# An adaLN layer on one core: the routed tiles' second products move to two banks of their own, and the feed-forward's first products end two tiles earlier

## What is computed

```python
h = layernorm(x) * (1 + ca) + sa
x = x + ga * attention(h)                     # 16 heads of 16, causal
h = layernorm(x) * (1 + cb) + sb
shared = silu(h @ w1.T) * (h @ w2.T) @ w3.T   # 1024 hidden
top2 = top_k(sigmoid(h @ router.T) + bias, 2) # 8 experts, 256 hidden each
routed = sum over the two experts of (silu(h1) * h2 * gate) @ w3[e].T
x = x + gb * (shared + routed)
```

## Time and profile before

| | us |
|---|---|
| runs (three) | 2202.20, 2202.41, 2206.81; median 2202.41 |
| the profiled execution, its own time | 2220.47 |
| its span, first to last instruction | 2218.6 |
| TensorE busy | 1999.8 (90%) |
| VectorE busy | 1626.2 (73%) |
| ScalarE busy | 1067.9 (48%) |
| GpSimd busy | 799.4 (36%) |
| mean granted TensorE clock | 0.953 of full |

### The profile page before, as it was taken

How to read it: one execution, slowest core, us unless ns; L and a number is a source line. 1 busy time by engine, 2 the same in 40 slices (tenths; PEclk the granted TensorE clock), 3 DMA queues, 4 the chain that set the end, 5 groups by cost and what they waited for, 6 DMA issues and landing times.

```text
span 2218.6 us, 47132 instructions
## 1 busy us (share of the span) xinstructions
PE 1999.8 (90%) x17686; PEld 1057.9 (48%) x17686; DVE 1626.2 (73%) x4438; ACT 1067.9 (48%) x1401; POOL 799.4 (36%) x811
## 2 busy tenths in 40 slices
PE   5778889999999899989999999999998988999995
PEld 2223334344444444434443444354444477788773
DVE  6887778776877697768777877787778366655475
ACT  1555544554555455545454545455553545444431
POOL 1110142133223422342234323322323447876653
PEclk8788889998999999999999999899998999999997
DMA  3246220102011201120202020102010446787696
GB/s 124 97 162 200 77 66 22 50 21 71 18 42 38 73 16 49 34 70 16 59 29 65 21 63 26 58 24 60 27 48 21 157 92 114 126 172 121 152 282 203
DMA packets 109661, 175.64 MB, mean 79 GB/s; under 512 B 14576, under 2 KB 80376, under 8 KB 108288
## 3 DMA queue, kind: packets, MB, share of 16 engines
q1 hardware_dynamic: 82848, 136.63, 20.5%
q0 software_dynamic: 26592, 36.00, 8.7%
HBM read 76.43 MB, written 70.44 MB: 66 GB/s over the span
## 4 chain that ended last, share of the span: by engine, by line
PE 60%; DVE 27%; ACT 4%; issue 3%; POOL 3%; DMA 2%; another core or an unknown queue 1%; SPq 1%; POOLq 0%; ACTq 0%; DVEq 0%
PE bank L1794 11%; DVE bank L1247 8%; DVE max_part L1241 8%; PE bank L1846 8%; PE bank L1826 6%; PE bank L1757 5%; PE bank L1709 5%; PE misc L1780 5%; PE bank L1733 4%; PE pv L1780 3%; PE bank L1837 3%; PE bank L1873 2%; PE bank L1719 2%; ACT arena L1050 2%; POOL sum L938 1%
## 5 line engine op out<-in xcount | busy, mean ns | idle before, releaser
L1050 ACT ACTIVATE arena<-bank 128x1024 f32<-128x1024 f32 (+1 forms) x640 | 592.8, 935 | 448.9 <-PE bank L1757 419.9
L1247 DVE CUSTOM_DVE_ANT_0 bank<-bank,mask 128x512 f32<-128x512 f32 (+3 forms) x1024 | 472.2, 520 | 69.1 <-PE bank L1733 58.3
L880 POOL TENSOR_SCALAR_AFFINE_SELECT arena<-arena 128x512 f32<-128x512 f32 x256 | 170.0, 671 | 711.5 <-ACT arena L1050 711.0
L1794 PE MATMUL bank<-feat_parts,ffn_sb 128*128 128x512 f16 x1536 | 371.8, 391 | 7.5 <-ACT arena L1050 3.2
L1241 DVE TENSOR_REDUCE max_part<-bank 128x2 f32<-128x1024 f32 x256 | 312.4, 1220 | 25.8 <-PE bank L1733 23.5
L1757 PE MATMUL bank<-arena 50*128 50x256 f16 (+1 forms) x2560 | 244.7, 271 | 69.7 <-DVE max_part L1241 23.2
L1733 PE MATMUL bank<-arena 48*128 48x512 f16 (+3 forms) x1536 | 233.3, 349 | 57.7 <-DVE max_part L1247 19.4
L938 POOL DMA_INDIRECT sum<-arena,feat x142 | 232.2, 1635 | 136.8 <-DVE arena L1473 65.5
L944 POOL TENSOR_TENSOR hidden<-silu_h,hidden 128x512 f16<-128x512 f32 x128 | 155.8, 1220 | 249.3 <-ACT hidden L1083 248.3
L1780 PE MATMUL misc<-arena,v_sb 128*32 128x256 f32 (+1 forms) x3072 | 236.9, 382 | 1.0 <-POOL arena L880 0.9
L1794 PEld LDWEIGHTS bank<-feat_parts,ffn_sb 128*128 128x128 f16 x1536 | 142.2, 100 | 199.7 <-issue 38.6
(11 more groups left out here) (211 smaller groups left out, 2476.6 us busy)
## 6 DMA issues: line engine op xcount, KB each, us to landing
arena<-parts SPq DMA_DIRECT2D x384, 64.0 KB, 2.2
feat<-lists SPq DMA_DIRECT2D x71, 265.0 KB
sum<-feat_parts SPq DMA_DIRECT2D x9, 1024.0 KB, 6.3
rows<-x SPq DMA_DIRECT2D x8, 1024.0 KB, 5.6
x_sb<-x SPq DMA_DIRECT2D x16, 512.0 KB, 6.5
sum<-norm SPq DMA_DIRECT2D x14, 512.0 KB, 3.3
ffn_parts<-hidden SPq DMA_DIRECT2D x8, 768.0 KB, 4.1
arena<-ffn_parts SPq DMA_DIRECT2D x8, 768.0 KB, 7.0
```

The costliest lines, as they stand in the source:

```text
L880: gp.affine_select(p, p, [[0, GH], [1, P]], ALU.is_ge, 0.0, 0, -1).then_inc(masked, 1)
L1050: sc.activation(to[:, :, lo:QC], of[:, :, lo:QC], ACT.Exp, scale=SCALE / QK_SCALE ** 2).then_inc(exp_done, 1)
L1247: last = vec.tensor_tensor_reduce(scored, scored, mask[:, 512 - nk:], scale=1.0, scalar=NEG, op0=ALU.add, op1=ALU.max, accum_out=max_part[ ...
L1794: last = mm(to[:, 512 * m:512 * m + 512], w_up[s][W_PART[i]][:, f, m * RH + h * P:m * RH + (h + 1) * P], feat_parts[:, A_PART[i], f, c * 5 ...
```

## The change

The y products of tile i (`ty`) no longer take a tile of the planned three; they go to `attended[i % 2]`, and TensorE waits for that bank's last reader by hand: for tiles 0 and 1 for the attention's last two steps, from then on for `y_ready` of tile i-2. `ty` goes out of BUSY and READ, so that the plan of all other steps in the end comes out anew. In that new plan the steady tiles alternate as xr(i+3) in the tile that tup(i) had, tup(i+2) in the one that xr(i+2) had; where before tup(i+2) followed tup(i+1), xr(i+3) followed xr(i+2) and ty(i) followed ty(i-1), each in its own tile. In the stretch with the router and the ranks the new plan gives tup(10) the tile of router 0 just ahead of it, tup(14) that of rank 0, tup(15) that of router 1, tup(19) that of rank 1 and tup(22) that of count 1 (the last as before); tup(8) keeps following tup(7).

LATE_FFN goes from 19 items to 22, spread over the tiles 52 to 68 instead of 52 to 70: all 16 ups and the last low part now lie ahead of ty(68), and four downs alone follow the last tile. The tiles 52, 55, 58, 62 and 65 get two items. `down` 0 comes in tile 58's step, behind tup(60) and ahead of ty(58); before it came in tile 61's, behind xr(64).

```diff
-LATE_FFN = len(END_FFN) - 7
+LATE_FFN = len(END_FFN) - 4
 FFN_FROM = 52
-FFN_AT = [FFN_FROM + n * (ALL_TILES - FFN_FROM) // LATE_FFN for n in range(LATE_FFN)]
+FFN_AT = [FFN_FROM + n * (ALL_TILES - 2 - FFN_FROM) // LATE_FFN for n in range(LATE_FFN)]
...
-            if n == 4:
+            if n == 1:
                 put([("own", 0)])
...
-        "qk": 46, "v": 46, "turn_out": 5, "max_turn": 8, "rank": 4, "count": 1, "mods": 60, "xr": 9, "tup": 28, "ty": 15}
+        "qk": 46, "v": 46, "turn_out": 5, "max_turn": 8, "rank": 4, "count": 1, "mods": 60, "xr": 9, "tup": 28}
...
-        "qk": 30, "v": 17, "max_turn": 14, "rank": 6, "count": 4, "mods": 16, "xr": 18, "tup": 18, "ty": 9}
+        "qk": 30, "v": 17, "max_turn": 14, "rank": 6, "count": 4, "mods": 16, "xr": 18, "tup": 18}
...
-                        out_tile(at[0], buffer_of(v, ("ty", at[0])))
+                        out_tile(at[0], attended[at[0] % 2])
...
-                elif kind == "ty":
-                    pe.wait_ge(y_ready, at_tile(at[0]))
...
-                        tile_down(at[0], take(b, v, ("ty", at[0])))
+
+                        i = at[0]
+                        if i < 2:
+                            pe.wait_ge(o_ready, at_step(B - 1, STEPS - 2 + i))
+                        else:
+                            pe.wait_ge(y_ready, at_tile(i - 2))
+                        tile_down(i, attended[i % 2])
```

## The result

The change makes the kernel slower: 2209.85 us against 2201.36 (medians of 20 runs each), ratio 1.0042 with a 95% interval of 1.0031 to 1.0052, so some 9 us. (One run of the kernel before took 5258.82 us; the median hardly feels it.) The forecast was 2200.0, with a range of 2192.5 to 2206.5.

A forecast was written before the change was run, and what follows sets the result against it. TensorE with VectorE, and close by GpSimd's chain of adds, bound tiles 12 to 30. Tile 67's add, 2164.07 + 12.95 + 1.0 - 4.5 = 2173.5, plus 42.7 gave 2216.2 profiled, 2200.0 us as median; range 2192.5 to 2206.5.

The forecast's parts named there:

- Part 1: New banks, tiles 0 to 25: 7.5 us faster by TensorE and VectorE alone, capped and taken as -4.5 us.
- Together 5.9: Tiles 0 to 25: us added because tup(10), tup(15), tup(14) and tup(19) stand right behind a router or rank.
- rival C: Slower: tups behind router, rank or count, tup(10) to tup(22), tie TensorE to VectorE's order; 2207.5 us, chance 0.13.
- The clock: Tiles 0 to 25: 1.7 us regained from a tup slowed by the lower clock after a 2.00 us wait.
- The cap of 4.5 us by the chain of adds: Around tile 21: GpSimd's unbroken adds limit the gain of the new banks to 1.0 + 3.5 us.
- Part 2: Steady tiles: no change, 0 us, since TensorE is full there.
- Part 3: Feed-forward among the tiles: down 0 waits 3.2 us for its low part in its new place, +1.0 us in all.
- Part 4: The tail: five ups moved ahead cost +12.95 us; from tile 67's add to the end 42.7 us against 54.5.
- The rule on descriptors: Tail adds: GpSimd can't write descriptors while VectorE holds the shared port; some 0.6 us more per pair, not summed.
- rival D: Tail adds or landings slower, first_loads 24 us after tile 67's add: 2204.6 us, no change, chance 0.15.
- B: Tiles 0 to 25: the cap doesn't hold, the full 7.5 to 13.4 us come, 2197.0 to 2191.1 us; chance 0.25.
- E: Tail: the 9.3 us idle was only a shadow of the loads, moved ups do nothing; 2198.9 us, chance 0.05.

The follow-up runs named there:

- e1: The change's banks and plan with the feed-forward schedule of before, against the kernel before: 2206.13 against 2196.90 us, ratio 1.0045.
- e5: The change plus a third buffer for the tiles' rows, against the kernel before: ratio 1.0002.
- e14: The new banks with the old feed-forward schedule and a third row buffer, without raised reading costs, against the kernel before: ratio 0.9992.
- e16: New banks, planner's reading costs of 45, third row buffer and old feed-forward schedule, against the kernel before: 2180.21 against 2200.04 us, ratio 0.9910.
- e2: The kernel before with only the change's feed-forward schedule, second products still in the ring of three: ratio to before 1.0010.
- e12: The kernel before with only a third buffer for the tiles' rows: ratio to before 0.9956.
- e9: The change with the planner's reading costs of router, rank and count raised to 45 in the end: 2198.85 us, ratio to before 0.9992.
- e17: The kernel before with the third row buffer and the planner's reading costs of 45, second products still in the ring: ratio to before 0.9962.

## Why the prediction was wrong

**Part 1 is the step that failed: -4.5 forecast, +7.9 measured** (e1: 9.2 us by the medians). TensorE's time from the first second product to tile 30's can be split into waits of over 0.15 us and the rest: 14.8 + 144.4 before, 21.0 + 146.1 after. By its terms:

- The old waits, 13.4 to go: right. 13.4 us of waits for L1461 and L1473 in this stretch became 0.5; the 1.7 that I left for the table was too cautious by 1.2.
- "Together 5.9" for the new waits behind readers: 12.3 in the trace; before had 1.0 at count 1 and 0.2 at rank 0, so 11.1 are new. Each tup's shift was priced rightly: tup(10) began 43.31 us after the first second product where it had begun 42.15, +1.2 (forecast +1.5), tup(14) 5.4 later (forecast 4.4 with tup(10)'s). What was wrong is the sum: I took the price once off the gain, while the gain itself was waited away as well. TensorE came early to each reader (tile 7's second products were 2.2 us ahead) and waited that lead away there. That is rival C, whose price was to be "twice that if what was gained is waited for again"; I gave it 0.13.
- The clock: I had booked 1.7 as won, since one wait of 2.00 us goes. But three tups now ran slow behind waits of 4.02, 3.66 and 2.26: 5.09, 3.94 and 4.29 us to the next second products where 2.62 is usual. The rest column says +1.7 lost net, 3.4 from my term.
- Row loads, 8.0 us in this stretch: absent from the sum. Before had one such wait, 2.1 us for tile 2's rows ahead of the first second product, and none behind it; it is the line that the earlier trace rows leaves out, `PE bank L1805 <- DMA feat<-lists: 2.1, 1, 2.1`. The prediction asked for the cover of the chain of adds and not for that of the loads, which hang on VectorE's copy of ids two tiles back. e5 and e14 show that they are a cost of their own, though a part of it comes back as other waits.

Together: 5.2 for the readers, 3.4 for the clock, 8.0 for rows, less 1.2, is 15.4, and from the -7.5 that I had for TensorE and VectorE alone that gives the measured +7.9.

- The cap of 4.5 us by the chain of adds: wrong, and it didn't show in the change only because nothing was won. In e16 tile 30 is 12.1 us earlier although tile 22's add is only 3.1 us earlier (127.7 against 130.8): two banks and four output buffers lie between them, and tile 30's add may come 14.5 us behind its second products. The steady tiles, 4.38 us each for TensorE and some 3.7 for a pair of adds, close the gap later.

**Part 2**, 0: the 21 steady tiles took 91.9 us instead of 92.8. Right within a microsecond.

**Part 3**, +1.0: the stretch from tile 51 to tile 67 grew by 14.3, 12.95 of it the ups, so +1.3. The wait of down 0 was 3.33 (forecast 3.2), against 2.47 in the earlier trace rows.

**Part 4**, the tail of 42.7: 44.3 was measured. first_loads started 19.1 after tile 67's add (forecast 19.4). What was off is the fifth load: I had the eight loads in one row by their rate, but the fifth waits for tile 70's add to land, and that took 6.83 us from its issue, beside the first four loads; the earlier trace rows have 4.72 for tile 68's in the kernel before. VectorE began its last eight instructions at +31.1 instead of +29.5. Ups and tail together cost +4.0 where I had +2.15; e2's ratio gives 2.2, its medians 4.2.

**The rule on descriptors.** The two adds of tile 68 took 1.82 and 2.08 us, those of tile 69 1.55 and 2.17, and both of tile 70's, with no output made beside them, 1.55. So pairs beside the output making are longer by 0.8 and 0.6 us; the forecast had some 0.6. Whether that is the rule's doing isn't shown: the Trainium skill (SBUF — State Buffer, the "DVE blocks DMA" trap) tells it of VectorE operations in a two-port mode, with a `tensor_copy` as its example, and the output making here is a `tensor_tensor`. These pairs took 3.88 and 3.76 us before and 3.90 and 3.72 after: it is no cost of the change, first_loads was on time, and rival D didn't come about.

**The other rivals.** B (no cap) was right about the cap, and its 13.4 us are nearly what e16 has at tile 30; but not in this kernel, because C came with it. E: fell, the tail from tile 67's add is 10.3 us shorter.

## What to carry to other kernels

When a change takes away a wait, look at every place further on where the same engine meets a second, slower one: here the lead was lost at each of them, so the new waits were not to be subtracted from the gain: they replaced it. List for each engine all that it waits for with the slack of each, loads with two buffers above all: a third buffer brought 8.8 us with the old banks (e12), and the new banks 11.1 on top of it, with the reading costs (e16). And a planner with costs for readers is only as good as those costs where the readers are themselves queued: 6 stood for the read alone, 45 for the place that it had in ScalarE's and VectorE's lists. Only these two values were run.

## What was unexpected of the hardware

A wait can cost more than itself. Behind the 4.02 us of tup(10) the granted clock was 0.51 for the next 6 us. In e9 TensorE stood only 0.75 and 1.46 us at that place, and the stretch ran at full clock:

```profile
1816.00:1822.00 6.00, 6.00 (x61) 5.27 (x60) 1.69 (x6) 5.57 (x7) 4.84 (x4) 1.00 0.91 153
```

With 2.03 us there, in e16, the same tiles had 0.74:

```profile
1810.00:1816.00 6.00, 5.89 (x45) 4.81 (x46) 1.68 (x5) 5.52 (x7) 4.85 (x4) 0.74 0.90 151
```

That the third row buffer pays in the ring of before (e12, e17: 0.9956 and 0.9962) was not expected either, and e12's trace explains 5.8 of its 8.8 us, 2.0 of them ahead of the first second product.
